# Attention layer of a four-layer graph network: edge and distance terms as two more features of each head

## What is computed

```python
q = (nodes @ Wq + bq).reshape(N, HEADS, HEAD_DIM)
k = (nodes @ Wk + bk).reshape(N, HEADS, HEAD_DIM)
scores = jnp.einsum('ehd,ehd->eh', q[src], k[tgt]) / np.sqrt(HEAD_DIM)
scores = scores + edges @ We + be
cons = jax.nn.sigmoid(jax.nn.relu(conservation_scores @ Wc1 + bc1) @ Wc2 + bc2)
scores = scores * cons[tgt]
scores = scores + jax.nn.relu(distances @ Wd1 + bd1) @ Wd2 + bd2
seg_max = jax.ops.segment_max(scores, tgt, num_segments=N)
w = jnp.exp(scores - seg_max[tgt])
```

## Time and profile before

| | |
|---|---|
| median of 3 runs | 7069.73 us (7066.88 to 7076.96) |
| the profiled execution's own time | 7046.59 us |
| its span | 7044.6 us |
| edge loop of the last layer (first to last gather) | 5680.4 to 6930.6 us of the span, 1250.2 us |
| busy over the whole span | PE 60%, PEld 39%, DVE 45%, ACT 12%, POOL 46% |

### The profile page before, as it was taken

The page is one execution under the profiler, slowest core; times in us unless marked ns, Lnnn a source line. Parts: engine busy times, 40 slices in busy tenths (PEclk is TensorE's granted clock), DMA queues, the critical chain, the costliest instruction groups (busy, mean ns, idle before and its releaser), DMA issues. The chain is left out here.

```text
span 7044.6 us, 85720 instructions
## 1 busy us (share of the span) xinstructions
PE 4200.1 (60%) x18026; PEld 2739.5 (39%) x18027; DVE 3150.8 (45%) x8308; ACT 856.9 (12%) x2517; POOL 3222.8 (46%) x3301
## 2 busy tenths in 40 slices
PE   6820111167799677777775658888788743333433
PEld 6800000022399544434434544444444432333322
DVE  6910011177698455555556771221121254444445
ACT  2200000011110021212111001010010012222221
POOL 0077777700000166666661004646646446666663
PEclk6555555588899777788787989898898955555555
DMA  4300000013367466666663546676575542223332
GB/s 122 88 17 11 11 2 2 11 49 90 121 246 274 149 183 173 184 172 179 174 181 92 146 121 239 220 238 219 206 253 202 182 126 71 70 73 73 74 71 58
DMA packets 564874, 910.99 MB, mean 129 GB/s; under 512 B 100563, under 2 KB 402664, under 8 KB 526004
## 3 DMA queue, kind: packets, MB, share of 16 engines
q1 hardware_dynamic: 459630, 742.44, 32.6%
q0 software_dynamic: 105024, 166.00, 10.5%
HBM read 677.34 MB, written 230.78 MB: 129 GB/s over the span
## 5 line engine op out<-in xcount | busy, mean ns | idle before, releaser
L2030 POOL DMA_INDIRECT l_edges_by_src<-l_by_src,src_i x816 | 786.5, 964 | 1495.5 <-POOLq L1764 1002.5
L3020 POOL DMA_INDIRECT l_gathered<-l_table,l_st x816 | 776.5, 952 | 1003.6 <-issue 833.6
L402 POOL DMA_INDIRECT by_src<-src_rec,src_pos x784 | 815.6, 1040 | 546.7 <-DVEq L315 290.4
L2030 POOL DMA_INDIRECT l_edges_by_src<-l_q,src_i x816 | 778.3, 954 | 563.4 <-DVE l_scores L3160 241.6
L3089 PE MATMUL psum<-l_blocks,l_rows 128*128 128x512 f32 (+1 forms) x2016 | 881.8, 583 | 75.7 <-issue 73.0
L2124 PE MATMUL psum<-l_rows,l_edges_hot_t 128*128 x1632 | 420.7, 433 | 792.7 <-DVE l_scores L3160 637.0
L1929 PE MATMUL psum<-pair_hot_weight,pair_hot_dst 128*128 128x512 f32 x1200 | 731.7, 754 | 176.5 <-DVE pair_hot_dst L1919 109.3
L2124 PEld LDWEIGHTS psum<-l_rows,l_edges_hot_t 128*128 128x128 f32 x1632 | 359.0, 313 | 861.9 <-issue 861.8
L1163 PE MATMUL psum<-hot_block,hot_low_src 128*128 128x400 bf16 x1136 | 338.1, 420 | 591.6 <-issue 295.9
L3048 DVE TENSOR_SCALAR l_hot<-iota,l_loc,l_weight 128x128 f32<-128x128 f32 x816 | 225.7, 357 | 1024.9 <-DMA pair_blocks<-pair_block 236.0
L1135 DVE TENSOR_SCALAR hot_block<-block_iota,visit_key 128x400 bf16<-128x400 f16 x1136 | 284.9, 322 | 812.9 <-remote 526.7
(11 more groups left out here) (561 smaller groups left out, 5223.6 us busy)
## 6 DMA issues: line engine op xcount, KB each, us to landing
l_blocks<-pair_blocks SPq DMA_DIRECT2D x216, 1024.0 KB
l_counts<-counts SPq DMA_DIRECT2D x67, 1600.0 KB, 7.1
pair_blocks<-pair_block SPq DMA_DIRECT2D x75, 1024.0 KB
l_edges_loc<-loc_by_tile SPq DMA_DIRECT2D x416, 128.0 KB
l_rows<-l_edges_by_src SPq DMA_DIRECT2D x204, 256.0 KB
l_sum_rows<-l_rows SPq DMA_DIRECT2D x204, 256.0 KB
counts<-count_rows SPq DMA_DIRECT2D x25, 1600.0 KB, 7.1
attr_space<-in_edge_attr SPq DMA_DIRECT2D x14, 1568.0 KB
```

The source lines that it names most:

```text
L402: pool.indirect_dma_start(table, bass.IndirectOffsetOnAxis(ap=pos[:, e:e + 1], axis=0), rec[:, e, :], None).then_inc(s_out[g % R], 16)
L2030: pool.indirect_dma_start(a[:, r, g, :], None, table_src, bass.IndirectOffsetOnAxis(ap=k.src_i[:, n * G + g:n * G + g + 1], axis=0))\
L3020: pool.indirect_dma_start(sent[:, p, g, :], None, by_type, bass.IndirectOffsetOnAxis(ap=st[:, p, g:g + 1], axis=0))\
```

## The change

The rows of a head become 18 numbers long: 16 features, then one column `ATTR` and one `DIST`. They are laid out feature by feature, that is 18 runs of 8 heads (144 numbers, `QD`), in the gathered row and in `krow`. In the query's row ScalarE puts the edge term into `ATTR` and the distance term into `DIST`, right into the ring `a`, beside the 128 numbers that the gather brings; `terms` is gone. In the key's row `ATTR` holds `cons` and `DIST` holds 1. The keys are multiplied by `cons` once for all nodes, behind the last window of `keep`, and the scale goes into the queries there. A score is then one product over 144 columns and one sum over 18 numbers that stand 8 apart. The product waits for the picks of its group.

```diff
@@ edge_rows
                 for g in range(G):
-                    pool.indirect_dma_start(a[:, r, g, :], None, table_src,
+                    pool.indirect_dma_start(a[:, r, g, 0:table_src.shape[1]], None, table_src,
...
                 if pick is not None:
                     act.wait_ge(s_done, n + 1)
                     act.nop(nofuse=True)
-                    pick(act, n, r, i)
+                    pick(act, n, r, i, a[:, r, :, D:])
@@ layer_attention
+    ATTR, DIST = C, C + 1
+    QD = D + 2 * HEADS
-        krow = k.sb(outer, "l3_rows", [P, W, D + HEADS])
+        krow = k.sb(outer, "l3_rows", [P, W, QD])
+        turned_heads = lambda ap: ap.rearrange("p w (c h) -> p w h c", h=HEADS)
+        krows, qrows = turned_heads(krow[:, :, :]), turned_heads(q)
-            terms = k.sb(ctx, "l3_terms", [P, R, G, 2 * HEADS])
...
             def consume(v, n, r, par, a, b):
                 here = s[:, par, r * G * HEADS:(r + 1) * G * HEADS].rearrange("p (g h) -> p g h", h=HEADS)
-                v.tensor_tensor(a, a, b[:, :, 0:D], ALU.mult).then_inc(s_p, 1)
+                v.wait_ge(s_terms, n * G + G)
+                v.nop(nofuse=True)
+                v.tensor_tensor(a, a, b, ALU.mult).then_inc(s_p, 1)
                 v.wait_ge(s_p, n + 1)
                 v.nop(nofuse=True)
-                v.tensor_reduce(here, a.rearrange("p g (h c) -> p g h c", c=C), AXX, ALU.add).then_inc(s_c, 1)
-                v.wait_ge(s_c, n * 3 + 1)
-                v.wait_ge(s_terms, n * G + G)
-                v.nop(nofuse=True)
-                v.scalar_tensor_tensor(here, here, float(C) ** -0.5, terms[:, r, :, 0:HEADS],
-                                       ALU.mult, ALU.add).then_inc(s_c, 1)
-                v.wait_ge(s_c, n * 3 + 2)
-                v.nop(nofuse=True)
-                v.tensor_tensor(here, here, b[:, :, D:D + HEADS], ALU.mult).then_inc(s_c, 1)
-                v.wait_ge(s_c, n * 3 + 3)
-                v.nop(nofuse=True)
-                return v.tensor_tensor(here, here, terms[:, r, :, HEADS:], ALU.add)
+                return v.tensor_reduce(here, a.rearrange("p g (c h) -> p g h c", h=HEADS), AXX, ALU.add)
...
                     def ends(v, step):
-                        step(v.tensor_copy(krow[:, :, D:D + HEADS], k.cons[:, :, :].rearrange("p h w -> p w h")))
+                        step(v.tensor_copy(krows[:, :, :, ATTR], k.cons[:, :, :].rearrange("p h w -> p w h")))
+                        step(v.memset(krows[:, :, :, DIST], 1.0))
+                        step(v.tensor_scalar(b[:, 2 * D:3 * D], b[:, 2 * D:3 * D], float(C) ** -0.5, None, ALU.mult))
...
                     def keep(v, n, ps):
                         v.tensor_tensor(val[:, n, :], ps[:, 0:D], b[:, 0:D], ALU.add)
-                        v.tensor_tensor(krow[:, n, 0:D], ps[:, D:2 * D], b[:, D:2 * D], ALU.add)
-                        return v.tensor_tensor(q[:, n, :], ps[:, 2 * D:3 * D], b[:, 2 * D:3 * D], ALU.add)
+                        of_heads = lambda ap, m: ap[:, m * D:(m + 1) * D].rearrange("p (h c) -> p h c", c=C)
+                        v.tensor_tensor(krows[:, n, :, 0:C], of_heads(ps, 1), of_heads(b, 1), ALU.add).then_inc(s_key, 1)
+                        ins = v.scalar_tensor_tensor(qrows[:, n, :, :], of_heads(ps, 2), float(C) ** -0.5, of_heads(b, 2),
+                                                     ALU.mult, ALU.add)
+                        if n + 1 == W:
+                            v.wait_ge(s_key, W)
+                            keys = krow[:, :, 0:D].rearrange("p w (c h) -> p w c h", h=HEADS)
+                            ins = v.tensor_tensor(keys, keys, bc(krow[:, :, D:D + HEADS].unsqueeze(2), [P, W, C, HEADS]),
+                                                  ALU.mult)
+                        return ins
...
-                def pick_terms(act, n, r, i):
+                def pick_terms(act, n, r, i, rows):
                     of = windows_of(act.value_load(k.win_i[0:1, bass.ds(n, 1)], min_val=0, max_val=W ** G - 1))
                     for g in range(G):
-                        act.copy(terms[:, r, g, :], of_tile[:, :, bass.ds(i + ((r * G + g) * TG + SHIFT) - of[g], 1)]
+                        act.copy(rows[:, g, :], of_tile[:, :, bass.ds(i + ((r * G + g) * TG + SHIFT) - of[g], 1)]
                                  .rearrange("p h a -> p (h a)")).then_inc(s_terms, 1)
-                edge_rows(k, "l3_edges", t_q, D, krow, D + HEADS, consume, finish, turned, run, pick=pick_terms,
+                edge_rows(k, "l3_edges", t_q, QD, krow, QD, consume, finish, turned, run, pick=pick_terms,
```

More of the change, by code:

```diff
@@ L3140, in layer_attention @@
             of_tile = k.sb(ctx, "l3_terms_by_tile", [P, 2 * HEADS, T + SHIFT])
-            terms = k.sb(ctx, "l3_terms", [P, R, G, 2 * HEADS])
-            s_p, s_c, s_terms = k.sem("l3_products"), k.sem("l3_score_steps"), k.sem("l3_terms_picked")
+            s_p, s_key, s_terms = k.sem("l3_products"), k.sem("l3_keys_made"), k.sem("l3_terms_picked")
             def consume(v, n, r, par, a, b):
                 here = s[:, par, r * G * HEADS:(r + 1) * G * HEADS].rearrange("p (g h) -> p g h", h=HEADS)
-                v.tensor_tensor(a, a, b[:, :, 0:D], ALU.mult).then_inc(s_p, 1)
+                v.wait_ge(s_terms, n * G + G)
+                v.nop(nofuse=True)
+                v.tensor_tensor(a, a, b, ALU.mult).then_inc(s_p, 1)
                 v.wait_ge(s_p, n + 1)
                 v.nop(nofuse=True)
-                v.tensor_reduce(here, a.rearrange("p g (h c) -> p g h c", c=C), AXX, ALU.add).then_inc(s_c, 1)
-                v.wait_ge(s_c, n * 3 + 1)
-                v.wait_ge(s_terms, n * G + G)
-                v.nop(nofuse=True)
-                v.scalar_tensor_tensor(here, here, float(C) ** -0.5, terms[:, r, :, 0:HEADS],
-                                       ALU.mult, ALU.add).then_inc(s_c, 1)
-                v.wait_ge(s_c, n * 3 + 2)
-                v.nop(nofuse=True)
-                v.tensor_tensor(here, here, b[:, :, D:D + HEADS], ALU.mult).then_inc(s_c, 1)
-                v.wait_ge(s_c, n * 3 + 3)
-                v.nop(nofuse=True)
-                return v.tensor_tensor(here, here, terms[:, r, :, HEADS:], ALU.add)
+                return v.tensor_reduce(here, a.rearrange("p g (c h) -> p g h c", h=HEADS), AXX, ALU.add)
             def finish(v, i, par):
```

## The result

The changed kernel takes 7103.89 us (median of 5 runs), the kernel before 7069.73: a ratio of 1.0052, with an interval of 1.0038 to 1.0065. The forecast was 6969 us, within 6845 to 7055. The profiled execution takes 7105.92 us, its span is 7104.1.

What follows compares the result with a forecast made beforehand. POOL was taken to bound the edge loop: 1008.5 us of gathers and issue plus 241.6 of waits. Waits falling to 135 us gave -107, work ahead of the loop +6, so -101: 6969 us, range 6845 to 7055.

Steps and rivals of the forecast that it cites:

- POOL's row: Last layer's edge loop: gathers and their issue, 1008.5 us, plus 241.6 us of waits for scores explain the whole 1250.1.
- Projection: Ahead of the loop: product over all keys, extra clearing and scaling, and strided sums add 6 us (4 to 9).
- the crawl: Edge loop: some 7 us after POOL starts, until it stops, other engines' small instructions go through only very slowly.
- a pause still has to last till the crawl has ended and the group is through, about 3.0 us: POOL's waits in the edge loop: each remaining pause lasts about 3.0 us, against a mean of 3.3 before.
- 45 x 3.0: POOL's waits in the edge loop: some 45 pauses of 3.0 us, 135 us instead of 241.6, 107 less.
- the 2.90 of one pause: Edge loop of the kernel before: one profiled POOL pause of 2.90 us, cited for the forecast pause of about 3.0.
- longer pauses: Rival for POOL's edge-loop waits: stretches of four groups each end in 6.5 us pauses, 332 us of waits, 7166; chance 0.07.
- the 4.7 from which it decides: POOL's edge-loop waits: mean pause in us, 241.6 / 51, from which the slower rival would decide.
- its own 6.5: POOL's edge-loop waits: pause length in us the slower rival assumed, 51 times, after one pause of 6.46 us.
- 9 x 88/128: Crawling groups in the edge loop: small instructions fall from 128 to 88 per body, so 9 us of gaps become 6.2.
- four to five groups per stretch: Edge loop: POOL pauses about every 4 to 5 groups instead of 2.8, some 45 times.

Runs made afterwards that it cites:

- g6_incs: The changed kernel with eight more small instructions per group on VectorE ahead of the product, each counting up a semaphore nobody waits for; ratio 1.0155.
- g1_direct: The changed kernel with plain POOL transfers of 128-row tiles in place of gathers by index in the last layer's edge loop; ratio 0.9111.
- e3_before_less: The kernel before without the three small operations on the scores and their waits, keeping the near sum and 512 columns; ratio 0.9977.
- e4_early: The changed kernel with its product written to PSUM over the key rows, so gathered rows are free after the product, not the sum; ratio 0.9941.
- e1: The changed kernel with its sum reading numbers side by side in place of 8 apart; ratio 1.0014.
- e2: The kernel before with its sum over 512 columns reading numbers 8 apart; ratio 0.9991.
- the variants on that chip: The changed kernel with eight empty instructions per group on VectorE, four per gather on POOL, or POOL only three groups ahead; ratios 1.0031 to 1.0046.
- g3_late_psum: The changed kernel with its product written to PSUM over the key rows, but POOL, picks and TensorE still released after the sum; ratio 1.0028.
- h5_early_ring2: e4_early with POOL allowed to run two groups ahead in place of four; ratio 0.994.
- h7_no_picks: The changed kernel without ScalarE's picks, their 16 columns cleared once ahead of the loop and the product not waiting for copies; ratio 0.9999.
- f1_before_early: The kernel before with its product written to PSUM over the key rows and gathered rows free after the product; ratio 0.9997.

## Why the prediction was wrong

**What held.** POOL's row does explain the loop: 783.8 + 233.2 + 271.1 = 1288.1. The sum takes 1.189 us (forecast 1.17), the product 0.751 (0.75). The pauses number 50 (45, with up to 51 in the range), but that is luck in part, as the second failed step shows. Projection +0.7 us, where +6 was forecast. The product over all keys took 3.48 us as priced, but it wasn't on the path: VectorE's idle time behind it, till the stores were through, went from 6.01 to 2.55 us. The dearer strided writes (377 and 393 ns for 279) cost little of the layer's start either. And the crawl is real: it begins some 4 to 8 us after POOL (7.8 in the stretch shown), falls on small instructions (g6_incs), comes from POOL's gathers by index (g1_direct), and ends soon after POOL stops (1 to 3 us in the means of the runs with picks).

**The step that failed** is "a pause still has to last till the crawl has ended and the group is through, about 3.0 us", in "45 x 3.0". It took the 2.90 of one pause, with one operation of 0.19 us left behind the crawl, over to a kernel in which more is left. Measured behind 16 gathers: 2.65 us till the crawl ends, and 2.80 for product, sum and restart, 5.45 in all; over all pauses 50 x 5.42 = 271.1. That is the rival "longer pauses", to which the prediction gave 0.07: the next group has nearly all its work ahead as POOL stops. 5.42 is over the 4.7 from which it decides; its own 6.5 was too much. The trace of the kernel before could have warned: its pauses were 2.37 us behind 8 gathers, 3.12 behind 12 and 6.60 behind the ten stretches of 16, while the forecast let the stretches grow to some 18 gathers (816 / 45) and kept the pause at 3.0. The mechanism is shown from both sides: e3_before_less gets the long pauses from the removal alone, and e4_early, which takes the sum out of what stands behind the crawl, brings 64 to 75 us back on the same chip.

**The second failed step** is "9 x 88/128": that a group with fewer small instructions crawls through sooner. The crawl doesn't hand its slots to VectorE in proportion. In the loop VectorE had 441 slow small instructions before and 135 after, while the four engines' sum rose from 1220 to 1402. In the crawl it didn't creep forward; in the stretch shown it stood at one wait for 9.4 us, from the end of its last register instruction (6275.40) to 6284.77. Before, its product and its sum came during the crawl but ahead of the pause in most stretches, and so cost POOL nothing. The forecast reached its four to five groups per stretch by way of a group that creeps through in 9 us; four came about, but not that way.

**What of the 0.5%.** From e3 (0.9977) to e1 (1.0014) are 26 us on the same chip. They belong to 64 more columns, the product's wait for the picks and the projection, which weren't tried apart; both projection (0.7 us) and wait for the picks look small in the trace. The far sum comes on top, dear here and free in the old order (e2): 12 to 23 us by the variants on that chip, 26 by g3_late_psum, 27 to 36 by the changed kernel's own ratios.

**Open.** How gathers by index slow the waits and register work of all engines is not settled, nor by what rule the slots are given out. The Trainium skill, "NOTIFIC — the notification-queue block", section "Overflow: three behaviours, one of which stalls the engine", says that the block which writes instruction records can hold back the engines, in one of its three ways of meeting a full ring. No run here shows that it did. What was slow here are instructions that leave a record, and the empty ones that leave none showed no cost, which would fit; but no run was made to part it. Nor do the times tell: the profiled execution (7105.92 us) is no longer than the others (7103.05 to 7107.91), and of none is it known that it ran without such records.

**The best version** found is e4_early, which beats both kernels: 0.9941 [0.9919, 0.9963]; h5_early_ring2 can't be told from it (0.994, on another chip).

## What to carry to other kernels

Where one engine is held up until another pauses, ask what stands between the end of the hold-up and the release, not how much work there is in all: shorten that piece, or release ahead of it, before taking work away elsewhere. A pause's length read from one order of work can't be carried to another; add it up anew from the place where the chain will stand. And a change of order and a change of amount are worth testing as a square: here each alone gave nothing or less, and both together 0.6%.

## What the runs showed of the hardware that I had not expected

- From some 4 to 8 us after POOL has started to issue gathers by index back to back, nearly every wait and register instruction of VectorE, ScalarE, TensorE and SyncE takes 0.70 us, on a common grid, till 1 to 3 us after POOL stops (means of these runs; h7_no_picks, without ScalarE's part, ends sooner): 1402 of the 8578 in the changed kernel's loop. Otherwise waits mostly take 0.02 to 0.05 and register work up to some 0.3. With plain transfers of POOL through the same loop at most 3 of some 8570 are slow.
- The sum of 576 numbers that lie 8 apart takes 1189 ns from SBUF and 758 from PSUM; side by side in SBUF it takes 753. From PSUM side by side 512 numbers take 692 (f1_before_early), which with 64 more columns at 1.04 ns is 759. So the distance costs 436 ns in SBUF and nothing in PSUM. The Trainium skill, "Advanced Engine Details and Errata", section "Memory Cachelines", says the first for SBUF's lines of 16 bytes, and the traces agree. For PSUM it names lines of 8 bytes and a slowdown of matmuls; on VectorE's sum no cost shows.
- An empty instruction asked for eight times per group on VectorE, or four times per gather on POOL, leaves no record, and no cost shows (1.0031 and 1.0046, for 1.0052 to 1.0065 without them on other chips).
